# Values and routing logits from one set of products with 144 columns, copied to SBUF in two fills

## What is computed

```python
xn = layernorm(x)
# attention: 16 heads of 8 channels, causal, scores and values through a 64-wide latent
s = attention(xn)                    # values = xn @ (W_dkv.T @ W_uv.T @ W_o.T)
# mixture of 8 experts, the two best of each token
logits = cos(xn, centroids) + xn @ w_route.T
gates = softmax(where(logits >= second largest, logits, -inf))
g = silu(sum_e gates[e] * (gelu(xn @ w1[e] + b1[e]) @ w2[e] + b2[e]))
x = x + s * g
# second layer: layernorm, keys/values/queries, a linear recurrence over the tokens, a sign-weight product, and again x + s * g
```

## Time and profile before

| | |
|---|---|
| Median of 3 runs | 754.84 us (754.81 to 756.4) |
| The profiled execution | 758.75 us, of which its span is 756.9 us |
| TensorE products / weight loads busy | 652.3 us (86%) / 452.7 us (60%) |
| VectorE, ScalarE, GpSimd busy | 445.2 us, 360.2 us, 236.8 us |
| Periods 3 to 7 | about 79.9 us each |

### The profile page before, as it was taken

How to read it: one execution, slowest core, us unless ns; L and a number is a source line. 1 busy time by engine, 2 the same in 40 slices (tenths; PEclk the granted TensorE clock), 3 DMA queues, 4 the chain that set the end, 5 groups by cost and what they waited for, 6 DMA issues and landing times.

```text
span 756.9 us, 14228 instructions
## 1 busy us (share of the span) xinstructions
PE 652.3 (86%) x5606; PEld 452.7 (60%) x5606; DVE 445.2 (59%) x1015; ACT 360.2 (48%) x680; POOL 236.8 (31%) x358
## 2 busy tenths in 40 slices
PE   4167698979999899989998999899989998896874
PEld 2034365447766676657665866576757775555763
DVE  5566457555857676676748675858575755225331
ACT  3502435754557445644566455645564546561210
POOL 5703101223433153124404341423332403125331
PEclk9999989979999999999999999999999999998995
DMA  2732620360035102520053004500350000000000
GB/s 69 135 70 43 133 60 8 90 106 7 6 82 102 35 2 65 93 68 1 29 107 83 8 8 105 105 7 9 93 96 17 1 7 16 21 1 1 0 15 14
DMA packets 31378, 36.32 MB, mean 48 GB/s; under 512 B 4433, under 2 KB 26608, under 8 KB 31312
## 3 DMA queue, kind: packets, MB, share of 16 engines
q1 hardware_dynamic: 31312, 35.42, 21.8%
HBM read 24.46 MB, written 9.96 MB: 45 GB/s over the span
## 4 chain that ended last, share of the span: by engine, by line
PE 61%; DVE 15%; ACT 6%; issue 6%; DMA 6%; POOL 4%; SPq 2%; POOLq 0%; DVEq 0%; ACTq 0%
PE ps_v L838 7%; PE ps_s L817 7%; PE ps_e L802 6%; DMA kst<-split_scratch 4%; DVE cand L1285 4%; PE ps_a L764 4%; PE ps_e L799 4%; PE ps_c L907 4%; PE ps_c L920 3%; PE ps_a L752 3%; PE ps_a L727 3%; DVE second L1230 2%; PE ps_s L821 2%; DVE xn L1230 2%; PE ps_c L924 2%
## 5 line engine op out<-in xcount | busy, mean ns | idle before, releaser
L1285 DVE TENSOR_REDUCE cand<-ps_s 128x4 f32<-128x512 f32 (+1 forms) x320 | 212.8, 682 | 89.1 <-PE ps_s L821 69.1
L1087 ACT ACTIVATE prob<-ps_e 128x512 f32<-128x512 f32 x320 | 188.1, 596 | 150.9 <-PE ps_e L802 149.2
L817 PE MATMUL ps_s<-kst,qst 96*128 96x128 bf16 (+1 forms) x1024 | 134.4, 249 | 40.7 <-DMA kst<-split_scratch 22.9
L817 PEld LDWEIGHTS ps_s<-kst,qst 96*128 96x128 bf16 x1024 | 82.2, 105 | 98.2 <-issue 50.1
L802 PE MATMUL ps_e<-qst,kst 128*128 128x384 bf16 (+3 forms) x512 | 124.5, 305 | 0.0
L799 PE MATMUL ps_e<-identb,negmask 128*128 128x256 bf16 (+1 forms) x320 | 83.2, 260 | 8.1 <-ACT prob L1087 8.1
L838 PE MATMUL ps_v<-prob,vaug 128*32 128x512 f32 (+3 forms) x1024 | 88.6, 441 | 0.0
L638 POOL TENSOR_TENSOR second<-second,upmask 128x512 f32<-128x512 f32 x42 | 53.0, 1269 | 31.9 <-PE ps_c L907 31.9
L802 PEld LDWEIGHTS ps_e<-qst,kst 128*128 128x128 bf16 x512 | 50.6, 99 | 5.8 <-issue 0.6
L601 POOL CAST mparts<-nm 128x32 bf16<-128x32 f32 x16 | 3.4, 210 | 151.7 <-DVE nm L1292 151.7
L907 PE MATMUL ps_c<-second 128*128 128x128 f32 x336 | 47.2, 285 | 1.2 <-POOL second L638 0.7
(11 more groups left out here) (304 smaller groups left out, 1045.2 us busy)
## 6 DMA issues: line engine op xcount, KB each, us to landing
qst<-split_scratch SPq DMA_DIRECT2D x48, 192.0 KB
kst<-split_scratch SPq DMA_DIRECT2D x144, 64.0 KB
split_scratch<-qparts SPq DMA_DIRECT2D x8, 384.0 KB, 2.5
split_scratch<-kparts SPq DMA_DIRECT2D x8, 384.0 KB, 2.5
xn<-in_L_attn_x_dram SPq DMA_DIRECT2D x8, 256.0 KB, 3.1
x_res<-in_L_attn_x_dram SPq DMA_DIRECT2D x8, 256.0 KB, 6.8
out_dram<-second SPq DMA_DIRECT2D x7, 256.0 KB, 2.4
max_scratch<-mrow SPq DMA_DIRECT2D x16, 96.0 KB, 1.7
```

What stands on the lines that cost most here:

```text
L817: last = mm(ps_s[:, bank, w * n:w * (n + 1)], q[0:MAXROW, hd, tok(i)], k[0:MAXROW, hd, keys[0]:keys[1]], start=(n == 0), stop=True, skip_g ...
L1087: af(prob[:, u, :], ps_e[:, u % 2, :], ACT.Exp).then_inc(S["e_emptied"], 1)
L1285: vec.tensor_reduce(cand[:, i, h0:h0 + FILLS * (len(hds) - 1) + 1:FILLS, S_SLOT[u]], ps_s[:, u % 2, :].rearrange("p (a c) -> p a c", a=len ...
```

## The change

The weights w_v (128 columns) and rwT (16 columns) become one tile w_vr of 144 columns, and the pieces `logits` and `v` of TensorE become `lv0` and `lv1`: two token tiles each, 144 columns each, 288 columns of ps_a in a fill. `lv0` stands at (1, 3), where `logits` stood, and `lv1` at (1, 4) behind `c_ffn`. ScalarE copies each fill to a new tile vl in SBUF. VectorE computes the logits from vl, in its piece `lv1`, when both copies are done. ScalarE's piece `v` stays in the tail and copies from vl instead of ps_a. `gates` moves from (1, 4) to (1, 5), behind `lev_a1`. The number of fills stays 17. The diff, cut to its core:

```diff
-A_XNT, A_Q, A_K = -11, -10, -9
-A_LOGIT, A_GT, A_M0, A_H, A_V = 3, 4, 5, 9, 13
+A_XNT, A_Q, A_K = -10, -9, -8
+A_LV, A_GT, A_M0, A_H = 3, 5, 6, 10
...
-    (1, 0): ["load_x", "c_kt", "c_qt", "m_rows1"], (1, 1): ["c_vk", "out"], (1, 2): ["c_gram", "pv2"], (1, 3): ["logits"],
-    (1, 4): ["yt", "c_ffn", "gates"], (1, 5): ["lev_a1"], (1, 6): ["pv0"], (1, 7): ["lev_d1"], (1, 8): ["gt"],
+    (1, 0): ["load_x", "c_kt", "c_qt", "m_rows1"], (1, 1): ["c_vk", "out"], (1, 2): ["c_gram", "pv2"], (1, 3): ["lv0"],
+    (1, 4): ["yt", "c_ffn", "lv1"], (1, 5): ["lev_a1", "gates"], (1, 6): ["pv0"], (1, 7): ["lev_d1"], (1, 8): ["gt"],
...
+        vl = sb("vl", [P, NT, VL])
...
-            def v(b):
-                a_fill(b, A_V)
-                for i in range(NT):
-                    last = mm(ps_a[:, tok(i)], xnT[b.parity][:, tok(i)], w_v[:, :], start=True, stop=True)
-                last.then_inc(S["a_filled"], 1)
-
-            def logits(b):
-                a_fill(b, A_LOGIT)
-                for i in range(NT):
-                    last = mm(ps_a[:, 16 * i:16 * i + 16], xnT[b.parity][:, tok(i)], rwT[:, :], start=True, stop=True)
+            def v_logits(b, half):
+                a_fill(b, A_LV + half)
+                for m in range(2):
+                    last = mm(ps_a[:, VL * m:VL * m + VL], xnT[b.parity][:, tok(2 * half + m)], w_vr[:, :], start=True, stop=True)
                 last.then_inc(S["a_filled"], 1)
...
-                        pe.wait_ge(S["v_ready"], b.count(1, 1))
-                        pe.wait_ge(S["a_emptied"], b.count(A_FILLS, a_number(b, A_V) + 1))
+                        pe.wait_ge(S["v_ready"], b.count(2, 2))
...
+            def v_logits(b, half):
+                a_full(b, A_LV + half)
+                after(act, S["v_ready"], b.count(2, 0))
+                if half == 0:
+                    after(act, S["top_ready"], b.count(NT, 0))
+                copy(vl[:, 2 * half:2 * half + 2, :], ps_a[:, 0:2 * VL].rearrange("p (i d) -> p i d", i=2)).then_inc(S["a_emptied"], 1)
+
             def v(b):
-                a_full(b, A_V)
+                act.wait_ge(S["a_emptied"], b.count(A_FILLS, a_number(b, A_LV + 1) + 1))
                 after(act, S["pv_used"], b.count(3 * GROUPS, 0))
-                by_turn = ps_a[:, :].rearrange("p (i h t d) -> p i h t d", i=NT, t=FILLS, d=HD)
-                copy(vaug[:, :, 0:HEADS:FILLS, 0:HD], by_turn[:, :, :, 0, :]).then_inc(S["v_ready"], 1)
-                copy(vaug[:, :, 1:HEADS:FILLS, FW:FW + HD], by_turn[:, :, :, 1, :]).then_inc(S["a_emptied"], 1)
+                for t in range(FILLS):
+                    copy(vaug[:, :, t:HEADS:FILLS, FW * t:FW * t + HD],
+                         vl[:, :, 0:P].rearrange("p i (h t d) -> p i h t d", t=FILLS, d=HD)[:, :, :, t, :]).then_inc(S["v_ready"], 1)
...
             def logits(b):
-                a_full(b, A_LOGIT)
+                dve.wait_ge(S["a_emptied"], b.count(A_FILLS, a_number(b, A_LV + 1) + 1))
                 dve.wait_ge(S["rn_ready"], b.count(1, 1))
...
-                vec.tensor_tensor(logit[:, :, :], lg[:, :, EXPERTS:2 * EXPERTS], coss[:, :, :], ALU.add).then_inc(S["a_emptied"], 1)
+                vec.tensor_tensor(logit[:, :, :], vl[:, :, P + EXPERTS:VL], coss[:, :, :], ALU.add).then_inc(S["logit_ready"], 1)
```

More of the change, by code:

```diff
@@ L29 @@
 VK = 128 + DS
+VL = 128 + 2 * EXPERTS
 LR = 0.01
@@ L112 @@
 PLAN_SECOND = ("load_x", "ln1_stats", "ln1_norm", "xnt", "q", "k", "stacks0", "stacks1", "zero")
-PLAN_NEXT = ("logits", "gates", "gt", "h0", "h1", "h2", "h3", "gelu", "v", "m_parts0", "m_rows0", "m_parts1")
+PLAN_NEXT = ("lv0", "lv1", "gates", "gt", "h0", "h1", "h2", "h3", "gelu", "v", "m_parts0", "m_rows0", "m_parts1")
 PLAN_OLDER = ("c_y2", "c_r3", "c_u3", "c_y3", "c_out")
@@ L219, in two_layers @@
         w_k = sb("w_k", [P, P])
-        w_v = sb("w_v", [P, P])
+        w_vr = sb("w_vr", [P, VL])
         rw = sb("rw", [2 * EXPERTS, P])
-        rwT = sb("rwT", [P, 2 * EXPERTS])
         cent_ss = sb("cent_ss", [EXPERTS, 1])
@@ L961, in c_y @@
                     mm(r.ps_c0[:, 0:P], r.vk[:, c, VK - P:VK], r.u_sb[:, :], start=True, stop=True).then_inc(r.S["c0_filled"], 1)
-            pieces = {"xnt": xnt, "q": lambda b: qk(b, 0), "k": lambda b: qk(b, 1), "v": v, "logits": logits, "gt": gt,
+            pieces = {"xnt": xnt, "q": lambda b: qk(b, 0), "k": lambda b: qk(b, 1), "lv0": lambda b: v_logits(b, 0), "lv1": lambda b: v_logits(b, 1), "gt": gt,
                       "out": out_piece, "m_rows0": lambda b: m_rows(b, 0), "m_rows1": lambda b: m_rows(b, 1), "pv0": lambda b, grp: pv(b, grp, 0), "pv1": lambda b, grp: pv(b, grp, 1), "pv2": lambda b, grp: pv(b, grp, 2), "yt": yt, "c_xn2t": c_xn2t, "c_ht": c_ht, "c_kt": c_kt,
@@ L999, in _ @@
             prep(6, keffT[:, :], ps_c1[0:KVL, 0:P])
-            prep(7, w_v[:, :], ps_c0[:, 0:P])
+            prep(7, w_vr[:, 0:P], ps_c0[:, 0:P])
             prep(8, perm_out(w_k[:, :]), perm(ps_a[:, 0:P]))
@@ L1134, in c_u @@
                 copy(r.u_sb[:, :], r.ps_c0[:, 0:P]).then_inc(r.S["c0_emptied"], 1)
-            pieces = {"xnt": xnt, "q": lambda b: split_hi(b, 0), "k": lambda b: split_hi(b, 1), "v": v, "gates": gates, "gt": gt,
+            pieces = {"xnt": xnt, "q": lambda b: split_hi(b, 0), "k": lambda b: split_hi(b, 1), "lv0": lambda b: v_logits(b, 0), "lv1": lambda b: v_logits(b, 1), "v": v, "gates": gates, "gt": gt,
                       "gelu": gelu, "out": out_piece, "m_rows0": lambda b: m_rows(b, 0), "m_rows1": lambda b: m_rows(b, 1), "pv2": pv, "c_xn2t": c_xn2t, "c_ht": c_ht, "c_kt": c_kt,
@@ L1238, in logits @@
             def logits(b):
-                a_full(b, A_LOGIT)
+                dve.wait_ge(S["a_emptied"], b.count(A_FILLS, a_number(b, A_LV + 1) + 1))
                 dve.wait_ge(S["rn_ready"], b.count(1, 1))
-                lg = ps_a[:, 0:2 * EXPERTS * NT].rearrange("p (i e) -> p i e", i=NT)
-                vec.tensor_tensor(coss[:, :, :], lg[:, :, 0:EXPERTS], bcast(rn[:, :], 2, EXPERTS), ALU.mult).then_inc(S["cos_ready"], 1)
+                vec.tensor_tensor(coss[:, :, :], vl[:, :, P:P + EXPERTS], bcast(rn[:, :], 2, EXPERTS), ALU.mult).then_inc(S["cos_ready"], 1)
                 dve.wait_ge(S["cos_ready"], b.count(1, 1))
-                vec.tensor_tensor(logit[:, :, :], lg[:, :, EXPERTS:2 * EXPERTS], coss[:, :, :], ALU.add).then_inc(S["a_emptied"], 1)
-                dve.wait_ge(S["a_emptied"], b.count(A_FILLS, a_number(b, A_LOGIT) + 1))
+                vec.tensor_tensor(logit[:, :, :], vl[:, :, P + EXPERTS:VL], coss[:, :, :], ALU.add).then_inc(S["logit_ready"], 1)
+                dve.wait_ge(S["logit_ready"], b.count(1, 1))
                 for i in range(NT):
@@ L1380, in _ @@
                       "ln1_norm": lambda b: ln_norm(0, b), "ln2_norm": lambda b: ln_norm(1, b), "ln3_norm": lambda b: ln_norm(2, b),
-                      "q": lambda b: split_rest(b, 0), "k": lambda b: split_rest(b, 1), "logits": logits, "gates": gates, "zero": zero_piece,
+                      "q": lambda b: split_rest(b, 0), "k": lambda b: split_rest(b, 1), "lv1": logits, "gates": gates, "zero": zero_piece,
                       "out": out_piece, "m_parts0": lambda b: m_parts(b, 0), "m_parts1": lambda b: m_parts(b, 1), "pv2": pv, "yt": yt, "c_vk": c_vk, "c_gram": c_gram, "c_ffn": c_ffn}
```

6 lines of the change are left out of this document (3 added, 3 removed).

## The result

The changed kernel takes **762.13 us**, median of 4 runs (760.89 to 763.92), against 755.35 us (754.81 to 756.4) for the kernel before beside it: a ratio of 1.008, 95% interval 1.0058 to 1.0103, so 4.4 to 7.8 us slower. The forecast was 760.0 with a range of 754.5 to 764.0.

What follows compares the result with a forecast made beforehand. The prediction took ScalarE to bound the tail, and TensorE without gaps and nearly full VectorE to limit step 1. Terms 0 + 2.4 + 1.1 + 1.4 + 0.3 = 5.2 us slower, 754.84 + 5.2 = 760.0 us, range 754.5 to 764.

Steps and rivals of the forecast that it cites:

- `v` leaving the tail gains nothing: Tail: removing 0.99 us of TensorE work, eight times, gains 0, as TensorE then waits for yT and ScalarE.
- One sign that the prediction named for being wrong: Tail: the forecast is wrong if yT's transposes start earlier than now against pv2.
- The 144 columns: Step 1, TensorE: the logits' 0.81 us becomes 1.05 for the two fills, 0.24 more, where TensorE has no cover.
- Copies of 0.40: Step 1, ScalarE: two new copies of 288 columns, 0.40 us each, in ScalarE's slack, the second on the logits' path.
- The gates 1.7 us later: Step 1, VectorE: later logits put dlt in period 6 at 431.35 instead of 429.67.
- 0.4 in `gt` in each of periods 3 to 8: Step 1: TensorE waits for gparts, 0.4 us a period (bounds 0 and 0.7), six times, 2.4 us.
- Periods 1 and 2: Ahead of `gt`, with little slack: later logits cost 1.4 us in period 1 and 1.1 in period 2.
- The wait of over 1 us in `gt`: Periods 1 and 2: sign expected in the profile after, `gt` newly waiting over 1 us for gparts.
- Copies to vaug from SBUF: Tail, ScalarE: reading SBUF instead of PSUM costs 28 ns per 128-column pass; two copies in six tails, 0.3 us.
- TensorE as the bound: Rival: TensorE bounds everywhere, so removed products gain 6.0 us, giving 748.8; chance 0.13.
- Absorbed delays: Rival: TensorE also arrives later, or a later wait swallows the rest; 0 to 1.5 us remain, 755.5; chance 0.15.
- A falling clock: Rival: longer tail gaps lower the granted clock, up to 2 us in each of five tails, 765 to 770; chance 0.05.

Runs made afterwards that it cites:

- e3: Kernel before, with piece v computing only one of four token tiles (copies stay): 755.82 us against 755.89 for the kernel before; period 79.87.
- e2: Kernel before, with only gates moved from (1, 4) to (1, 5) behind lev_a1: 756.82 us against 755.89 for the kernel before; period 79.81.
- e5: Changed kernel, with only gt moved from (1, 8) to the head of (1, 9): 758.26 us against 756.77 for the kernel before; period 80.02.
- e1: Changed kernel, with gates back at (1, 4) behind lv1: 762.56 us against 755.89 for the kernel before; period 80.54.
- e4: Changed kernel, with the two copies from vl to vaug on GpSimd instead of ScalarE: 760.15 us against 755.89 for the kernel before; period 80.17.
- e7: Kernel before, with gates at (1, 5) behind lev_a1 and gt at (1, 9): 754.26 us against 756.77 for the kernel before; period 79.50.
- e6: Changed kernel, with lv0 at (1, 2), lv1 at (1, 3), gates at (1, 4): 768.09 us against 756.77 for the kernel before; period 81.36.
- e9: Kernel before, with ScalarE copying the 64 logit columns to SBUF for VectorE: 764.56 us against 756.89 for the kernel before; period 81.30.
- e10: Changed kernel, early fills, late gt, vaug copies on GpSimd, whose two mask products wait for the logits: 758.85 us against 756.89 for the kernel before.

## Why the prediction was right, and where not

The time, 762.13, is in the range and on the forecast side. The mechanism was right in the tail and in the later gates; where in step 1, and in periods 1 and 2, the time is lost it had partly wrong. Up to the gelu of period 8 the changed kernel had lost 6.1 us in the profiles (639.04 against 632.91), and the last stage took 0.8 less than in the profile of before, which by the scatter above says nothing of the change. By the prediction's own steps:

1. **`v` leaving the tail gains nothing: right.** The transposes wait 0.81 for yT, and e3 shows it apart. One sign that the prediction named for being wrong did come, the transposes earlier against pv2, by 0.10 us: `v` itself had held them that long beyond yT. It gained nothing, since ScalarE is late behind it, and the wait for prob grew instead.
2. **The 144 columns: 0.24 taken, 0.18 measured.** The fills take 0.49 and 0.50 from start to start (430.89 to 431.38, 432.88 to 433.38), 0.99 instead of 0.81.
3. **Copies of 0.40: right** (0.39 and 0.40), in ScalarE's slack: from the first fill to the scores of unit (1, 6) TensorE takes 3.98 us (430.89 to 434.87) instead of 3.80 (425.93 to 429.73), which is the 0.18 of the fills and nothing for the copies.
4. **The gates 1.7 us later: right**, 1.69.
5. **0.4 in `gt` in each of periods 3 to 8: right in size, place and cause, but not the whole balance.** It is 0.36, it comes with the late place of the gates (e2 has it too), and e5 gives 0.31 of it back. The balance of period 6 is +0.07 from the tail, +0.18 for the fills, +0.36 in `gt`, -0.35 because the maximum ahead of unit (1, 7) is no longer behind the gates, and +0.20 because the one ahead of unit (1, 8) is (1.83 us from scores to scores instead of 1.63): 0.46, as measured. Steps 5 and 7 came to 0.45, with the 0.24 of step 2 taken as made up for by an earlier arrival. The prediction had named the fourth term as "some tenths earlier" and the fifth in its bound of 0.7, and gave neither a number of its own, so that its sum fits to a hundredth is luck in part. It also did not separate the place of the gates from the lateness of the logits: by e2 the place alone costs nothing (-0.06), and what costs is the logits that wait for both fills and their copies.
6. **Periods 1 and 2: 1.4 and 1.1 taken.** From the first fill to the transposes it takes 1.60 longer in period 1 (6.31 before, 7.91 after) and 1.12 in period 2 (5.54 and 6.66). That is near the terms, but the place was wrong. The wait of over 1 us in `gt` did not come: it is 0.31 and 0.19. The delay stands mostly ahead of it, in the fills (1.12 us each in period 1, where the logits took 1.73 in all) and in the scores' waits for the maxima behind the logits and the gates (in period 1 1.09 instead of 0.65). Period 2, first before, then after:

```profile
120.21 0.39 PE L817 MATMUL ps_s<-kst,qst 96*128 96x256 bf16 x2 [0.20 <-DVE cand L1285]
```

```profile
123.81 0.39 PE L812 MATMUL ps_s<-kst,qst 96*128 96x256 bf16 x2 [1.11 <-DVE cand L1285]
...
124.72 0.40 PE L741 MATMUL ps_a<-identb,gparts 128*96 128x128 bf16 x4 [0.19 <-POOL gparts L595]
```

So moving `gt` (e5) could bring little there. Between the waits for the stacks' transfers the periods grew by 1.47 and 1.68, so these waits hid nothing, as said. How much of that is chance stays open: e3, whose `v` is hidden there as well, differs from the kernel before by +0.3 and -0.5 in these stretches. So the tenths by which e1, e4 and e5 differ can't be read there.
7. **Copies to vaug from SBUF: 0.05 a tail taken, 0.07 measured** (from the gelu to the table 401.46 to 403.99, 2.53, after and 396.56 to 399.02, 2.46, before). By the fixed costs on the Trainium skill's page VectorE: DVE Perf Modes, section "The TRN2 errata — SBUF-src ops pay a fixed extra latency per instruction", cited in the prediction, it would be 0.09, an estimate. The measurement lies between the two.

What the sum lacked, 0.9 of the 6.1 us, is 0.65 in periods 1 and 2 (3.15 against 2.5 summed) and 0.42 us by which the changed kernel was already late when the first scores began (41.78 against 41.36), behind a wait for a transfer; this start ranged from 40.6 to 41.8 over the profiles. The lower end of the prediction's own range, 757, is 0.6 below what its terms give (754.84 + 1.1 + 1.4 + 0.3 = 757.6); nothing hangs on it.

The rivals: TensorE as the bound fell with e3. By the rule in the Trainium skill, Perfetto Trace Analysis, "Identifying the Most-Contended Engine", the engine with the highest occupancy is optimized first, and the change served TensorE, the busiest; the traces don't bear the rule out here, since its 4.0 us less gained nothing. Absorbed delays: not in period 6, where from the transposes of `gt` to the next gelu it is 42.53 us before and after, so that nothing lost in step 1 is made good. A falling clock: no, the granted clock is 1.00 in the windows from 240 to 560 us after as before, and its mean over the span is 0.976 after and 0.967 before.

## What to carry to other kernels

Find out what an engine waits for right behind the work that you take away from it: if it is another engine's result, the work was free. When a result on a chain of small operations comes later, moving the chain mostly chooses who waits for it (0.36 in `gt` against 0.35 for the maximum); move the one who needs it, if it has slack (e5: 0.31 us a period back; e7, with both moves: 0.37 less than before). And measure a repeated stretch inside the profile when the whole run scatters more than the effect.

## What was not expected of the hardware

In these traces a small VectorE operation whose two inputs both lie in SBUF does not run beside GpSimd's products with a mask; it lasts until the product beside it ends. For the two operations of the logits 0.19 us became 0.72 and 1.20 (e6) and 1.18 and 1.19 (e9), and 0.19 again once GpSimd waited (e10). With one operand in PSUM `logit` runs through, 0.19, beside the same product (427.15, above). The changed kernel escapes this narrowly: its coss, in period 6 at 434.32, took 0.23 in periods 4 to 7, and GpSimd's products end at about 434.5. Staging the logits in SBUF therefore had a price that showed only when they were moved. The Trainium skill, SBUF — State Buffer, section "Who interferes with whom", has a rule for this: a VectorE instruction with two SBUF inputs takes its second one through a read interface that it shares with GpSimd, the shared ports are an exclusive lock, and the order of issue decides who is blocked. The traces agree in the one direction that they show, VectorE waiting for GpSimd.
